# Last MLP chunk: values and gates in one product, unused events dropped, transposes read the token buffer

## The reference, cut to what matters

```python
def attn_layer(x, Wqkv, qs, ksc, Wo):
    qkv = x @ Wqkv                       # 256 -> 3 * 1024
    q, k, v = jnp.split(qkv, 3, -1)      # 16 heads of 64, l2norm, scales, rotary tables
    ...
    return out @ Wo
def ffn_layer(x, g, bln, W1, b1, W2, b2):
    xn = (x - mu) / jnp.sqrt(var + 1e-05) * g + bln
    hg = xn @ W1 + b1                    # 256 -> 2 * 682
    a, gate = jnp.split(hg, 2, -1)       # values, gates
    return a * jax.nn.gelu(gate, approximate=False) @ W2 + b2
for i in range(6):
    x = attn_layer(shift_tokens(x), ...) + x
    x = ffn_layer(shift_tokens(x), ...) + x
```

## Time and profile before

| | us |
|---|---|
| median of 3 runs | 5054.81 (5049.03 to 5055.35) |
| the profiled execution, its own time | 5053.79 |
| its span in the trace | 5051.9 |
| last stage's steps, first transpose to last product | 1966.5 to 5016.4 |
| one body in mid-stage | 124.74 |
| TensorE busy in the span | 4704.6 (93%) |
| DVE, ACT, POOL busy | 3066.8, 2708.8, 1196.4 |

### The profile page before, as it was taken

The page is one execution under the profiler, slowest core; times in us unless marked ns, Lnnn a source line. Parts: engine busy times, 40 slices in busy tenths (PEclk is TensorE's granted clock), DMA queues, the critical chain, the costliest instruction groups (busy, mean ns, idle before and its releaser), DMA issues. The chain is left out here.

```text
span 5051.9 us, 90018 instructions
## 1 busy us (share of the span) xinstructions
PE 4704.6 (93%) x31376; PEld 2908.3 (58%) x31376; DVE 3066.8 (61%) x10717; ACT 2708.8 (54%) x6891; POOL 1196.4 (24%) x763
## 2 busy tenths in 40 slices
PE   4779999888899998999999999999999999999995
PEld 2446666555555554666666666666666666666653
DVE  1341222555666666877777777777777777777763
ACT  1212221545455454766666666666666666666661
POOL 0000000000000002533333333333333333333320
PEclk9999999999999999999999999999999999999997
DMA  4000000000000001001010111010101110101001
GB/s 143 13 13 0 0 0 26 14 1 0 26 1 14 14 1 43 24 18 44 26 35 18 44 26 35 18 44 26 35 18 44 28 36 18 44 26 35 18 14 36
DMA packets 78445, 128.58 MB, mean 25 GB/s; under 512 B 13666, under 2 KB 48212, under 8 KB 77652
## 3 DMA queue, kind: packets, MB, share of 16 engines
q1 hardware_dynamic: 78036, 123.28, 8.3%
HBM read 68.74 MB, written 4.19 MB: 14 GB/s over the span
## 5 line engine op out<-in xcount | busy, mean ns | idle before, releaser
L454 PE MATMUL psum<-f_wqkv,f_xsT 128*128 128x512 f32 x2304 | 1076.5, 595 | 4.1 <-ACT f_raw L591 2.7
L806 POOL TENSOR_TENSOR f_raw<-f_rot 128x512 f32<-128x512 f32 x384 | 487.8, 1270 | 1777.4 <-DVE f_rot L666 1777.4
L605 ACT ACTIVATE f_prob<-f_prob,f_nb,f_rq 128x128 f32<-128x128 f32 x1536 | 740.3, 489 | 9.5 <-DVE f_nb L715 8.7
L707 DVE CUSTOM_DVE_ANT_0 f_prob<-psum,f_band 128x128 f32<-128x128 f32 x1536 | 356.3, 287 | 526.7 <-issue 412.5
L454 PEld LDWEIGHTS psum<-f_wqkv,f_xsT 128*128 128x128 f32 x2304 | 400.7, 191 | 322.5 <-issue 318.0
L553 PE MATMUL psum<-f_xnT,f_w 128*128 128x512 f32 (+1 forms) x1152 | 525.5, 596 | 1.8 <-ACT f_xnT L626 1.1
L811 POOL TENSOR_TENSOR f_rn<-f_ss,f_half_pow 128x32 f32<-128x32 f32 x96 | 522.3, 5440 | 11.1
L589 ACT ACTIVATE f_sq<-psum 128x512 f32<-128x512 f32 x384 | 229.6, 598 | 255.6 <-PE psum L454 255.5
L730 DVE TENSOR_SCALAR f_prob<-f_prob,f_rs 128x128 f32<-128x128 f32 x1536 | 351.0, 292 | 13.7 <-DVE f_rs L724 0.2
L553 PEld LDWEIGHTS psum<-f_xnT,f_w 128*128 128x128 f32 (+1 forms) x1152 | 197.7, 179 | 275.5 <-issue 272.9
L536 PE MATMUL psum<-f_wo,f_oT 128*128 128x256 f32 x1536 | 350.1, 381 | 2.4 <-ACT f_v L591 1.5
(11 more groups left out here) (252 smaller groups left out, 8797.5 us busy)
## 6 DMA issues: line engine op xcount, KB each, us to landing
f_v_near<-f_v SPq DMA_DIRECT2D x168, 256.0 KB, 3.7
f_wqkv<-in_Wqkv SPq DMA_DIRECT2D x36, 512.0 KB, 6.0
w_moe_W<-in_L_ffn_W SPq DMA_DIRECT2D x2, 4096.0 KB
f_w<-in_W SPq DMA_DIRECT2D x6, 1364.0 KB, 5.6
f_wo<-in_Wo SPq DMA_DIRECT2D x6, 1024.0 KB, 6.7
f_xs<-x_all SPq DMA_DIRECT2D x24, 254.0 KB
x_srcT<-in_ctxT SPq DMA_DIRECT2D x8, 512.0 KB, 3.8
x_mask_int<-in_mask_BxSxS_ik SPq DMA_DIRECT2D x4, 1024.0 KB, 6.3
```

The source lines that it names most:

```text
L454: mm = nc.tensor.matmul(ps.ap(step), xsT[:, c, t * P:(t + 1) * P], wqkv[:, c, i * HALF:(i + 1) * HALF], start=c == 0, stop=c == KC - 1)
L605: ex = nc.scalar.activation(pr, pr, ACT.Exp, bias=nb[:, t % 2, h:h + 1], scale=rq8[:, t, h:h + 1], accum_out=sums[:, t % 2, h:h + 1])
L707: red = nc.vector.tensor_tensor_reduce(prob[:, (4 * n + 2 * j + i) % 16, :], ps.ap(key)[:, j * P:(j + 1) * P], band[:, min(t, 1), :], 1.0, ...
L806: nc.gpsimd.tensor_tensor(raw[:, (4 * t + i) % 8, :], rot[:, n % 2, 0, :], rot[:, n % 2, 1, :], ALU.add).then_inc(rope_done, 1)
```

## The change

Four edits in the last stage:

1. The gates' last chunk (42 columns) and the values' last chunk (42 columns) become one product `f1p` of 128 stationary columns. `w1` in SBUF is laid out anew: values 0 to 681, a gap, the gates' last 42 columns at 704, a gap, and the full gate chunks from 768. In PSUM the values come out on partitions 0 to 41, the gates on 64 to 105. ScalarE's gelu reads the latter and writes `hT[0:42]`, with the bias from a new tile `b1g_last`. A new DVE step `f1b` in slot 15 then reads the values from the same bank and drains it.
2. The weights `W1` are loaded in three DMAs instead of one, plus one for `b1g_last`, so every wait for them counts 128 instead of 80. The gaps are cleared once by DVE, and SyncE waits for that (`gaps_cleared`) before the first load.
3. `scores_clear`, `passed` and `xin_ready` are gone.
4. `xin` is gone, tile, copy and step. The transposes read `x_all`, and wait for `x_ready`.

The ring of banks gets `f1p` in place of the gates' last chunk, and nothing in place of the values' last chunk: 43 products in a body.

```diff
-        self.w1 = ctx.enter_context(nc.sbuf_tensor("f_w1", [P, KC, 2 * self.HID], F32))
+        self.w1 = ctx.enter_context(nc.sbuf_tensor("f_w1", [P, KC, (2 * self.HC - 1) * P], F32))
...
-        sp.dma_start(self.w1[:], w["W1"][l].rearrange("(c p) n -> p c n", p=P)).then_inc(self.w1_landed, 16)
+        sp.dma_start(self.w1[:, :, 0:self.HID], source[:, :, 0:self.HID]).then_inc(self.w1_landed, 16)
+        sp.dma_start(self.w1[:, :, full + P:], source[:, :, self.HID:self.HID + full]).then_inc(self.w1_landed, 16)
+        sp.dma_start(self.w1[:, :, full + W:full + W + self.HREM], source[:, :, self.HID + full:]
+                     ).then_inc(self.w1_landed, 16)
...
+        sp.dma_start(self.b1g_last[W:W + self.HREM, :], w["b1g"][l][0:self.HREM, :]
+                     ).then_inc(self.w1_landed, 16)
...
-                    4: [("xin", 1), ("tab", 1, 0)], 5: [("f2", -2, 2)], 6: [("f2", -2, 3)],
+                    4: [("tab", 1, 0)], 5: [("f2", -2, 2)], 6: [("f2", -2, 3)],
...
-                    14: [("f1g", -1, 4), ("f1g", -1, 5)],
-                    15: [("f1a", -1, 4), ("f1a", -1, 5), ("wo", 0, 2)]}.get(n, ())
+                    14: [("f1g", -1, 4), ("f1p", -1)],
+                    15: [("f1a", -1, 4), ("f1b", -1), ("wo", 0, 2)]}.get(n, ())
...
-            elif kind in ("qkv", "wo", "f2", "f1g", "f1a"):
+            elif kind in ("qkv", "wo", "f2", "f1g", "f1a", "f1p"):
...
+            sp.wait_ge(gaps_cleared, 1)
             weights.load_w1(sp, 0)
...
-                        pe.wait_ge(xin_ready, it + off + 1)
-                        transposes(step, it, [(t, xin[:, t, c * P:(c + 1) * P]) for t in range(TB)])
+                        pe.wait_ge(x_ready, it + off + 1)
+                        transposes(step, it, [(t, x_all[:, tile(it + off, t), c * P:(c + 1) * P]) for t in range(TB)])
...
-                        pe.sem_inc(scores_clear, 1)
...
+                    elif kind == "f1p":
+                        pe.wait_ge(ps.sem_drained(step), ps.before(step, it))
+                        for c in range(KC):
+                            mm = nc.tensor.matmul(ps.ap(step), w1[:, c, (HC - 1) * P:HC * P], xnT[:, c, :],
+                                                  start=c == 0, stop=c == KC - 1)
+                        mm.then_inc(ps.sem_filled(step), 1)
...
+                    elif kind == "f1p":
+                        wait_filled(act, ps, step, it)
+                        nc.scalar.activation(hT[0:HREM, HC - 1, :], ps.ap(step)[W:W + HREM], ACT.Gelu,
+                                             bias=weights.b1g_last[W:W + HREM, HC - 1:HC]).then_inc(gate_ready, 1)
...
+            nc.vector.memset(w1[:, :, (HC - 1) * P:HC * P], 0.0).then_inc(gaps_cleared, 1)
...
-                            dve.sem_inc(passed, 1)
...
+                    elif kind == "f1b":
+                        key = ("f1p", off)
+                        dve.wait_ge(gate_ready, it + off + 1)
+                        nc.vector.scalar_tensor_tensor(
+                            out=hT[0:HREM, HC - 1, :], in0=ps.ap(key)[0:HREM], scalar=b1a[0:HREM, HC - 1:HC],
+                            in1=hT[0:HREM, HC - 1, :], op0=ALU.add, op1=ALU.mult).then_inc(ps.sem_drained(key), 1)
...
-                        nc.gpsimd.tensor_copy(xin[:], x_all[:, bass.ds(j % NB * TB, TB), :]).then_inc(xin_ready, 1)
```

More of the change, by code:

```diff
@@ L245, in stage_l1_ffn @@
         xn_ready = sem("xn_ready")
+        gate_ready = sem("gate_ready")
+        gaps_cleared = sem("gaps_cleared")
         x_ready = sem("x_ready")
@@ L410, in one_body @@
                     copy_near(ps, it, 1, 1)
-                if b == 0 and has(("f1a", -1, HC - 1)) and has(("s", 0, 0)):
-                    wait_drained(sp, ps, ("f1a", -1, HC - 1), it)
+                if b == 0 and has(("f1p", -1)) and has(("s", 0, 0)):
+                    wait_drained(sp, ps, ("f1p", -1), it)
                     weights.load_w1(sp, l)
-                    announce(w1_weights, 80, l)
+                    announce(w1_weights, 128, l)
+            sp.wait_ge(gaps_cleared, 1)
             weights.load_w1(sp, 0)
@@ L545, in _ @@
                         if kind == "f1g" and ch == 0:
-                            pe.wait_ge(w1_weights, (it + off + 1) * 80)
+                            pe.wait_ge(w1_weights, (it + off + 1) * 128)
                             for c in range(KC):
                                 wait_drained(pe, ps, ("xnt", off, c), it)
-                        m = P if ch < HC - 1 else HREM
-                        at = (kind == "f1g") * HID + ch * P
+                        at = (kind == "f1g") * HC * P + ch * P
                         pe.wait_ge(ps.sem_drained(step), ps.before(step, it))
                         for c in range(KC):
-                            mm = nc.tensor.matmul(ps.ap(step)[0:m, :], w1[:, c, at:at + m], xnT[:, c, :],
+                            mm = nc.tensor.matmul(ps.ap(step), w1[:, c, at:at + P], xnT[:, c, :],
+                                                  start=c == 0, stop=c == KC - 1)
[4 more added lines that the diff above has]
+                            mm = nc.tensor.matmul(ps.ap(step), w1[:, c, (HC - 1) * P:HC * P], xnT[:, c, :],
                                                   start=c == 0, stop=c == KC - 1)
@@ L559, in _ @@
                             pe.wait_ge(w2_weights, (it + off + 1) * 48)
-                            wait_drained_in_last_body(pe, ps, ("f1a", -1, HC - 1), it)
+                            wait_drained_in_last_body(pe, ps, ("f1p", -1), it)
                         pe.wait_ge(ps.sem_drained(step), ps.before(step, it))
@@ L629, in _ @@
                         ch = step[2]
-                        m = P if ch < HC - 1 else HREM
                         wait_filled(act, ps, step, it)
-                        nc.scalar.activation(hT[0:m, ch, :], ps.ap(step)[0:m], ACT.Gelu,
-                                             bias=b1g[0:m, ch:ch + 1]).then_inc(ps.sem_drained(step), 1)
+                        nc.scalar.activation(hT[:, ch, :], ps.ap(step), ACT.Gelu,
+                                             bias=b1g[:, ch:ch + 1]).then_inc(ps.sem_drained(step), 1)
+                    elif kind == "f1p":
+                        wait_filled(act, ps, step, it)
+                        nc.scalar.activation(hT[0:HREM, HC - 1, :], ps.ap(step)[W:W + HREM], ACT.Gelu,
+                                             bias=weights.b1g_last[W:W + HREM, HC - 1:HC]).then_inc(gate_ready, 1)
         @block.vector
@@ L761, in _ @@
                         ch = step[2]
-                        m = P if ch < HC - 1 else HREM
                         if ch == 0:
-                            dve.wait_ge(w1_weights, (it + off + 1) * 80)
+                            dve.wait_ge(w1_weights, (it + off + 1) * 128)
                         wait_drained(dve, ps, ("f1g", off, ch), it)
@@ L767, in _ @@
                         nc.vector.scalar_tensor_tensor(
-                            out=hT[0:m, ch, :], in0=ps.ap(step)[0:m], scalar=b1a[0:m, ch:ch + 1],
-                            in1=hT[0:m, ch, :], op0=ALU.add, op1=ALU.mult).then_inc(ps.sem_drained(step), 1)
+                            out=hT[:, ch, :], in0=ps.ap(step), scalar=b1a[:, ch:ch + 1],
+                            in1=hT[:, ch, :], op0=ALU.add, op1=ALU.mult).then_inc(ps.sem_drained(step), 1)
+                    elif kind == "f1b":
[4 more added lines that the diff above has]
+                            in1=hT[0:HREM, HC - 1, :], op0=ALU.add, op1=ALU.mult).then_inc(ps.sem_drained(key), 1)
                     elif kind == "f2":
@@ L788, in _ @@
                     kind, off = step[:2]
-                    if kind == "xin":
-                        j = it + off
-                        pool.wait_ge(x_ready, j + 1)
-                        nc.gpsimd.tensor_copy(xin[:], x_all[:, bass.ds(j % NB * TB, TB), :]).then_inc(xin_ready, 1)
-                    elif kind == "tab":
+                    if kind == "tab":
                         pair = slice(2 * step[2], 2 * step[2] + 2)
```

13 lines of the change are left out of this document (5 added, 8 removed).

## The result

The changed kernel takes 5163.85 us (median of 4 runs, 5160.76 to 5166.13) against 5052.61 us for the kernel before, measured beside it (4 runs, 5049.03 to 5055.35): a ratio of 1.022, 95% interval 1.0202 to 1.0238. It is 2.2% slower; the forecast was 5158 us. The profiled execution took 5162.55 us, its span is 5160.6.

What follows compares the result with a forecast made beforehand. TensorE's products were taken to bound each body. 5053.79 + 48.2 (wait) + 1.3 (last body) + 50.6 (clock) + 4.6 (start) - 1.2 (tail) = 5157.3 us, told as 5158; range 5103 to 5182, the forecast's own 5130 to 5182.

Steps and rivals of the forecast that it cites:

- Products removed: In each body of the MLP stage: fewer products and the wider load win 1.96 us, 47 us over 24 bodies.
- The wait: Before wo 2: TensorE idles 3.96 us until f1b drains bank 0; body grows 2.19 us, 48.2 us over 22.
- The clock: After each new wait before wo 2: TensorE works at the lower clock level, losing 2.2 us, 50.6 us over 23.
- The range's upper end: Whole kernel: the forecast time's upper limit, 5182 us, said to take 3.1 us of clock per wait.
- Rule and trace: MLP stage's steady part: by the skill's rule on cycling PSUM banks the clock's term stands, some 5158 us; without it 5107.
- The wait alone: Rival, before wo 2: the wait comes but no clock is lost, 5107 us; chance 0.11.
- My aside: Before wo 2: with f1b about 1.2 us sooner, the wait would be short enough that the clock may hold.
- Hidden: Rival, before wo 2: DVE reaches f1b early enough that bank 0 is free, 5012 us; chance 0.05.
- Start: At the stage's start: the save of x_all leaves later, delaying DVE's first rotary step, 4.6 us; bounds 2 and 6.
- Tail: In the stage's tail: the second MLP product follows f1b directly after f1a 4, -1.2 us.
- Events and copy: On TensorE, DVE and GpSimd: dropping the increments and the copy into xin changes the time by 0.
- The sum: Whole kernel: all terms added to the profiled execution's 5053.79 us give 5157.3 us, told as 5158, 2% slower.

Runs made afterwards that it cites:

- e3_f1b_after_r: The changed kernel with DVE's f1b moved right behind step r of slot 14, after the products with the probabilities: 5034.62 us, ratio 0.9961.
- e1_ring44: The changed kernel with one bank skipped where f1b stands, so wo 2 is on bank 1 again: 5018.18 us, ratio 0.9931.
- e2_f1b_first: The changed kernel with DVE's f1b moved ahead of the reciprocal in slot 14, wo 2 still on bank 0: 5009.88 us, ratio 0.9910.
- e5_events_xin_only: The kernel before with only the increments dropped and transposes reading the token buffer without the copy into xin: 5051.44 us, ratio 0.9997.

## Why the prediction came out as it did

The mechanism was right in each step, the sum 5 us low. The clock's term alone was 10 us too low; that the total is nearer has partly to do with luck, as the last item shows.

- **Products removed, 1.93 and 0.03 us a body.** Right: without a wait the body is 122.73 us, 2.01 less than before; four records a body went.
- **The wait, 2.19 us a body, in 22 bodies.** Right: 3.98 us of idle time where 3.96 was forecast, ended by DVE's 42-row instruction, and no second wait. `f1b` ends where the old instruction ended, relative to the reciprocal, and TensorE needed 0.15 us after it, not 0.1. Without the clock the body grew by 2.17 us. That the ring makes it, and nothing else, is shown from both sides: taken out it leaves 5018 us, put into the kernel before it gives 5121. The last body's wait is 3.11 us.
- **The clock, 2.2 us for each wait.** The mechanism right, the size too small: this is the term that was off. Summed over the 23 low stretches TensorE worked 121.2 us at the lower level, so it lost 60.6 us, 2.63 a wait, where 50.6 were forecast. I took four waits as a sample, two followed by some 3 us of slow work and two by 6, and went under their mean. In the steady part they are not a mixture. The first two waits are followed by 2.97 and 3.41 us of slow work, the third by 5.35, and from the fifth on by 5.5 to 5.6, each time the same: 2.8 us lost, and 124.74 + 2.19 + 2.79 = 129.72 is the body. The range's upper end does not follow from its own working: 3.1 us of clock per wait give 5158 - 50.6 + 71 = 5178, not 5182.
- **Rule and trace.** The Trainium skill ("TensorE: Matmul & The Clock Gate", section "A second HAM failure mode: psum-queue depth-cycling") says of a bf16 kernel that cycles its PSUM banks with short idle times between groups of products that its clock goes down and up again while the median product looks fast. The trace of this float32 kernel agrees for the wait of 3.98 us: the mean clock of a body is 0.97, and the slow work is 5.6 us of 126. With the wait of 0.74 us (`e3_f1b_after_r`) it does not happen.
- **The wait alone, 5107.** Refuted for a wait of 4 us: all 23 (22 of 3.98 us, one of 3.11) were followed by the lower level. At 0.74 us none was, at 2.3 and 2.5 us about half. My aside, that a wait 1.2 us shorter might leave the clock alone, is half true: 1.4 us shorter, the clock still fell behind 10 of 22. The trace of the kernel before had said as much: of its 23 waits of 2.0 to 2.9 us, eight had a low stretch that began from 0.4 us ahead of their end to 1.5 us behind it.
- **Hidden, 5012.** Not what the change does, but what it could have done: 5010 and 5018 us were measured once the drain or the bank was moved. The condition named there (`f1b` ready 4 us sooner) is the one that decides.
- **Start, 4.6 us.** 4.45 measured at DVE's first rotary step, for the reason given: the save stands behind eleven issues that now wait for DVE's clearing. The absolute times were off by 2.4 us. That the whole of it goes through was wrong: at the first wo 1 that follows an MLP product 3.56 us are left (210.56 us behind the first clearing against 207.00); 0.6 of the rest went where TensorE's one wait for `f_xn` shrank from 1.2 to 0.6 us.
- **Tail, -1.2 us.** Right: 1.50 us in place of 2.69, the gap between the two value instructions is gone.
- **Events and copy, 0.** Right within what the time can tell (0.9997, 0.9988 to 1.0006 when made alone). TensorE's event records did not even become fewer: see below.
- **The sum.** From the forecast's 5157.3 to the measured 5162.55 it is +5.3 us: +10.0 for the clock, -2.4 for the stages before this one, -1.0 for the start, -0.6 for the growth of the bodies, and -0.7 behind the last wo 2, which took 115.18 us to the end against 115.34 before, though 1.7 us of the clock's loss fall there. That these four have the other sign is luck.

The body of `e1_ring44` is 0.30 us longer than that of `e2_f1b_first`. Its late wo 2 accounts for 0.22, and the other 0.08 lie in wo 2 itself: after the pause its second record starts 0.29 us behind its first, without a pause 0.22; the rest of the two bodies agrees to 0.01 us. What stays open is why a first product after a pause has that distance, and what the clock's falls follow.

## What to carry to other kernels

Taking one step out of a static ring of buffers shifts the buffer of every later taker (here of one, since the ring starts anew with each body): list for each who held it last and where its drain stands in the draining engine's queue, before counting what the removed step saves. If a taker now meets a drain that is queued late, move the drain (here into an idle gap of its engine, 154 us) or skip a buffer (146 us). A wait of 4 us between dense products cost 1.7 times its length here (3.98 us and 2.8 of clock), so that a body, instead of becoming 2 us shorter, became 5 longer.

## What the runs showed of the hardware beyond this

- A regular kernel can settle into the bad case of the clock. The body's length went 128.40, 128.63, 129.59, 129.64, 129.67 and stayed at 129.69 to 129.72. From the third wait on the low stretch is 6.8 us long, and it begins ahead of wo 2, first by 1.48 us and in the end by 1.23 to 1.25. In the kernels with waits of 2.3 and 2.5 us the low stretches are 3.4 us long, cost 1.6 to 1.7 us, and come behind about every second of waits that are alike. Why the longer wait gives double stretches I can't show.
- Removing increments did not remove TensorE's event records. Those at the scores, the wait's line and the increment's line before, then the wait's line after the change:

```profile
L478 PEldq EVENT_SEMAPHORE  x192: 51/51/51, 1994.9 to 4926.0; - x192
L479 PEldq EVENT_SEMAPHORE  x384: 51/51/427, 1995.0 to 4930.4; - x192
```
```profile
L484 PEldq EVENT_SEMAPHORE  x576: 51/51/1660, 1995.3 to 5038.8; - x192
```

  The earlier trace rows has only the second of these lines. 192 + 384 = 576: the records are as many as before, and what was put down to the increments now stands on the line of the waits. `e5_events_xin_only` has 576 as well, and its body is 124.74 us like the one before. So the 19.6 us that the 384 records add up to were never there to be had by dropping the increments. On DVE records did go: its lines have 2568 event records in the whole kernel before and 2133 with the change.
